# Graph attention, four layers: columns laid out by bits, marks of 0 and -1 as the penalty, and another order of the row tiles

## The reference

```
Wh = x @ W                                  # 4096 x 64
e = leaky(Wh @ a_src [:, None] + Wh @ a_dst [None, :])
scores = where(adj > 0, e, very negative)
out = softmax(scores, axis=1) @ Wh          # + bias in layer 1, elu in layers 0, 2, 3
x = layernorm(x + out)
```

## Time and profile before

| | |
|---|---|
| median of three runs | 632.23 us |
| the profiled execution | 631.51 us |
| its span, first to last instruction | 628.5 us |
| flag set, end of preparation | 216.00 us in the span |
| VectorE busy in the span | 426.0 us (68%) |
| GpSimd busy | 355.6 us (57%) |
| adjacency loads | 32 of 2048 KB |
| gathers | 340 |

### The profile page before, as it was taken

How to read it: one execution, slowest core, us unless ns; L and a number is a source line. 1 busy time by engine, 2 the same in 40 slices (tenths; PEclk the granted TensorE clock), 3 DMA queues, 4 the chain that set the end, 5 groups by cost and what they waited for, 6 DMA issues and landing times.

```text
span 628.5 us, 10864 instructions
## 1 busy us (share of the span) xinstructions
PE 358.2 (57%) x3424; PEld 318.5 (51%) x3424; DVE 426.0 (68%) x1856; ACT 364.8 (58%) x797; POOL 355.6 (57%) x354
## 2 busy tenths in 40 slices
PE   2363422313321279985189777527977762797773
PEld 1252311212221279884179776427867652786663
DVE  2898879899999845898135667713566761356686
ACT  3564865767664067985067657407766740675573
POOL 0200476266675740006777777767777777777770
PEclk9999999999999999998589879858997975998796
DMA  7996999999992110001122222212222221222220
GB/s 264 429 395 260 360 377 403 422 409 411 409 405 79 26 16 1 19 19 48 33 27 28 37 46 45 46 32 28 29 37 44 46 46 30 28 38 35 44 38 29
DMA packets 22083, 86.73 MB, mean 138 GB/s; under 512 B 6851, under 2 KB 12102, under 8 KB 17798
## 3 DMA queue, kind: packets, MB, share of 16 engines
q1 hardware_dynamic: 10102, 73.40, 29.0%
q0 software_dynamic: 10880, 11.51, 12.9%
q10 hardware_dynamic: 1040, 1.08, 0.5%
HBM read 80.59 MB, written 5.37 MB: 137 GB/s over the span
## 4 chain that ended last, share of the span: by engine, by line
POOL 32%; DVE 18%; issue 12%; PE 7%; ACT 4%; DMA 2%; POOLq 0%; DVEq 0%; ACTq 0%
POOL xg L404 32%; PE bank L601 2%; PE bank L575 2%; DVE key L1106 2%; DVE arena L1079 1%; DMA xg<-table,index 1%; DVE stats L1131 1%; ACT arena L716 1%; DVE nbr L879 1%; DMA table<-wh 1%; DVE mean_var L1134 1%; DVE key L1128 1%; DVE penalty L999 1%; ACT arena L734 1%; DVE key L1115 1%
## 5 line engine op out<-in xcount | busy, mean ns | idle before, releaser
L404 POOL DMA_INDIRECT xg<-table,index x340 | 333.9, 982 | 172.6 <-issue 100.7
L716 ACT ACTIVATE arena<-bank,sloped_own 128x256 f32<-128x256 f32 (+3 forms) x144 | 76.9, 537 | 150.1 <-PE bank L575 149.6
L1079 DVE CUSTOM_DVE_ANT_0 arena<-bank,arena 128x256 f32<-128x256 f32 (+3 forms) x144 | 71.5, 499 | 132.5 <-ACT arena L716 132.0
L690 ACT ACTIVATE arena<-arena,half 128x4096 bf16<-128x4096 int32 x32 | 118.4, 3707 | 46.9 <-DMA arena<-in_adj_t 46.3
L575 PE MATMUL bank<-packed,xg 128*128 128x128 f32 x744 | 120.0, 300 | 0.0
L575 PEld LDWEIGHTS bank<-packed,xg 128*128 128x128 f32 x744 | 113.2, 216 | 2.3
L601 PE MATMUL bank<-xg,arena 128*128 128x64 f32 x744 | 105.2, 280 | 11.6 <-ACT arena L734 11.0
L601 PEld LDWEIGHTS bank<-xg,arena 128*128 128x128 f32 x744 | 98.6, 202 | 17.2 <-ACT arena L734 16.5
L572 PE MATMUL bank<-penalty,ident_b 128*128 128x256 bf16 (+3 forms) x144 | 48.7, 338 | 75.6 <-DMA xg<-table,index 70.9
L725 ACT ACTIVATE arena<-arena,neg_max 128x256 f32<-128x256 f32 (+3 forms) x144 | 81.2, 564 | 0.3 <-DVE neg_max L1088 0.3
L588 PE MATMUL bank<-packed,arena 128*128 128x128 f32 x372 | 65.9, 284 | 10.2 <-ACT arena L734 9.1
(11 more groups left out here) (128 smaller groups left out, 522.4 us busy)
## 6 DMA issues: line engine op xcount, KB each, us to landing
arena<-in_adj_t SPq DMA_DIRECT2D x32, 2048.0 KB, 12.2
xg<-table,index POOLq DMA_INDIRECT x340, 2.8
table<-wh SPq DMA_DIRECT2D x24, 132.0 KB, 1.9
table<-wh ACTq DMA_DIRECT2D x1, 1056.0 KB, 4.7
x<-in_x SPq DMA_DIRECT2D x1, 1024.0 KB, 10.5
out_x<-x SPq DMA_DIRECT2D x8, 128.0 KB, 1.9
slot_row<-in_c_slot_row SPq DMA_DIRECT2D x1, 384.0 KB, 10.7
packed<-in_c_packed SPq DMA_DIRECT2D x1, 359.0 KB
```

What stands on the lines that cost most here:

```text
L404: pool.indirect_dma_start(out=xg[:, c, :], out_offset=None, in_=table[l][0:rows, :], in_offset=bass.IndirectOffsetOnAxis(ap=index[:, c:c + ...
L690: nc.scalar.activation(masks[:, t % 2, :], arena[:, t % 3, :], ACT.Sign, bias=half[:, :]).then_inc(mask_made, 1)
L716: nc.scalar.activation(score[:, n % RING, 0:m * P], score_ps[n % len(score_ps)][:, 0:m * P], ACT.Relu, bias=sloped_own[:, k:k + 1], scale= ...
L1079: nc.vector.tensor_tensor_reduce(out=y, in0=score_ps[n % len(score_ps)][:, 0:m * P], in1=y, scale=1.0, scalar=MASKED, op0=ALU.add, op1=ALU ...
```

## The change

- **The order of the batches.** Tiles 20-23 and 24-27 come first, then tile 0, then 1-3 and the rest as before. `GATHER_START` stays 2, which is now tile 0's batch.
- **The layout of columns.** The transposed adjacency is arranged on the host so that bit b of word w is column 256 b + w of the table's order. The count becomes three columns of each code group (low, high, all), so that a group is 11 wide in place of 9. For parted tiles VectorE sums two of the three over all 32 groups.
- **Candidates without column numbers.** The word gets a mark (bit 30) by one OR, and one AND with `bit_mask` puts mark, bit and word into a value whose order as a float is that of the columns. GpSimd's product (L398) and VectorE's L972 are gone. After the picking three small instructions turn the values into columns: `above`, `bit_col` and `col`.
- **Marks.** `slot_rows` makes `off_row` of 0 (the row's slot) and -1 (not): one comparison and one `scalar_tensor_tensor` a tile, one and three for parted tiles. It is kept for all batches and serves as the penalty itself: the matmul at the start of a segment takes `wall` (1e30 on the diagonal) and `off_row`. The penalty pass (L999) is gone. In `lists` each matmul becomes two, one with ones and one with `off_row`.

```diff
-BATCHES = [(0, 1), (20, 4), (24, 4), (1, 3), (4, 4), (8, 4), (12, 4), (16, 4), (28, 2), (30, 2)]
+BATCHES = [(20, 4), (24, 4), (0, 1), (1, 3), (4, 4), (8, 4), (12, 4), (16, 4), (28, 2), (30, 2)]
...
-                nc.gpsimd.tensor_tensor(colv[:, 0:places * BITS].rearrange("p (r b) -> p r b", b=BITS),
-                                        word_f[:, 0:places].unsqueeze(2).broadcast_to(wide),
-                                        bit_next[:, :].unsqueeze(1).broadcast_to(wide), ALU.add).then_inc(col_made, 1)
...
-                            t = nc.tensor.matmul(list_ps[q % 2][:, (c - c0) * w:(c - c0 + 1) * w],
-                                                 inrow[:, at:at + P],
-                                                 nbrh[:, b % 2, (k - k0) * w:(k - k0 + 1) * w],
-                                                 start=(k == tiles[0]), stop=(k == tiles[-1] and k0 >= PARTED))
+                            nc.tensor.matmul(dst, ones_b[:, :], rows, start=(k == tiles[0]), stop=False)
+                            t = nc.tensor.matmul(dst, off_row[:, at:at + P], rows, start=False,
+                                                 stop=(k == tiles[-1] and k0 >= PARTED))
...
-                    nc.tensor.matmul(bank[:, 0:m * P], ident_b[:, :], penalty[:, at:at + m * P],
+                    nc.tensor.matmul(bank[:, 0:m * P], wall[:, :], off_row[:, at:at + m * P],
...
-                    nc.vector.tensor_reduce(deg_part[:, 0, j:j + 1], both[:, 0:LOW, WORDS_C], AX, ALU.add)
-                    done(nc.vector.tensor_reduce(deg_part[:, 1, j:j + 1], both[:, LOW:TILES, WORDS_C], AX, ALU.add), j)
+                    nc.vector.tensor_reduce(deg_part[:, 0, j:j + 1], both[:, :, WORDS_C], AX, ALU.add)
+                    done(nc.vector.tensor_reduce(deg_part[:, 1, j:j + 1], both[:, :, WORDS_C + 1], AX, ALU.add), j)
...
-                        nc.vector.tensor_scalar(begun[:, at:at + w], slot_row[:, 0:w], first[:, j:j + 1], 0.0,
-                                                ALU.add, ALU.is_gt)
-                        t = nc.vector.tensor_scalar(ended[:, at:at + w], slot_row[:, 0:w], last[:, j:j + 1], 0.0,
-                                                    ALU.add, ALU.is_gt)
-                    link(t)
-                    return nc.vector.tensor_tensor(dst[:, 0:total], begun[:, 0:total], ended[:, 0:total], ALU.subtract)
+                        if rest is None:
+                            t = nc.vector.tensor_scalar(out, slot_row[:, 0:w], edges[:, j:j + 1], 1.0, ALU.is_lt, ALU.add)
+                        else:
+                            t = nc.vector.scalar_tensor_tensor(out=out, in0=slot_row[:, 0:w], scalar=edges[:, j:j + 1],
+                                                               in1=rest[:, at:at + w], op0=ALU.is_lt, op1=ALU.subtract)
+                    return t
...
+                if k0 < PARTED:
+                    link(mark(sooner, 0, low_start))
+                    link(mark(off_low, 0, low_end, sooner))
+                    link(mark(sooner, 0, start, off_low))
+                else:
+                    link(mark(sooner, 0, start))
+                mark(off_row, PLACE[k0] * P, end, sooner).then_inc(slots_made, 1)
...
-                nc.vector.tensor_scalar(lane_of[:, 0:places], topi[:, 0:places], GROUP - 1, None, ALU.bitwise_and)
-                done(nc.vector.tensor_scalar(word[:, 0:places], topi[:, 0:places], WORDS - GROUP, 4,
-                                             ALU.bitwise_and, ALU.logical_shift_left))
+                done(nc.vector.tensor_scalar(topi[:, 0:places], topi[:, 0:places], MARK, None, ALU.bitwise_or))
                 ready()
-                done(nc.vector.tensor_tensor(word_f[:, 0:places], word[:, 0:places], lane_of[:, 0:places],
-                                             ALU.add), None, word_made)
-                done(nc.vector.tensor_tensor(bitv[:, 0:places * BITS].rearrange("p (r b) -> p r b", b=BITS),
+                done(nc.vector.tensor_tensor(cand[:, 0, 0:places * BITS].bitcast(I32).rearrange("p (r b) -> p r b", b=BITS),
...
-                v.wait_ge(col_made, b + 1)
-                done(nc.vector.scalar_tensor_tensor(out=cand[:, 0, 0:places * BITS], in0=bitv[:, 0:places * BITS],
-                                                    scalar=0.0, in1=colv[:, 0:places * BITS], op0=ALU.is_gt,
-                                                    op1=ALU.mult), None, col_used)
...
+                done(nc.vector.tensor_scalar(above[:, 0:places], nbr[:, 0:places], -2.0, None, ALU.add))
+                ready()
+                done(nc.vector.tensor_scalar(bit_col[:, 0:places], above[:, 0:places].bitcast(I32), 15, 0xFF00,
+                                             ALU.logical_shift_right, ALU.bitwise_and))
+                ready()
+                done(nc.vector.scalar_tensor_tensor(out=col[:, 0:places], in0=nbr[:, 0:places].bitcast(I32),
+                                                    scalar=WORDS - 1, in1=bit_col[:, 0:places],
+                                                    op0=ALU.bitwise_and, op1=ALU.bitwise_or))
...
-                nc.vector.tensor_scalar(penalty[:, PLACE[k0] * P:PLACE[k0 + n] * P],
-                                        inrow[:, 0:(PLACE[k0 + n] - PLACE[k0]) * P], 1.0, -MASKED,
-                                        ALU.subtract, ALU.mult).then_inc(penalty_made, 1)
```

More of the change, by code:

```diff
@@ L191, in gat_kernel @@
         topi = sb("topi", [P, MAXB], I32)
[L192 to L196, removed]
+        above = sb("above", [P, MAXB], F32)
+        bit_col = sb("bit_col", [P, MAXB], I32)
+        col = sb("col", [P, MAXB], I32)
         cand = sb("cand", [P, 2, MAXB * BITS], F32)
@@ L207, in gat_kernel @@
         from_end = sb("from_end", [P, TILES], F32)
[L208 to L212, removed]
+        sooner = sb("sooner", [P, MAXBC * P], BF16)
+        off_low = sb("off_low", [P, MAXBC * P], BF16)
+        off_row = sb("off_row", [P, PLACE[TILES] * P], BF16)
+        wall = sb("wall", [P, P], BF16)
         rank = sb("rank", [P, 2, MAXBC], F32)
@@ L804, in _ @@
             v.wait_ge(loaded, 16 * NLOAD)
-            for dst, src in [(packer, packer_f), (fix, fix_f), (ones_b, ones), (before, before_f), (ident_b, ident)]:
-                t = nc.vector.tensor_copy(dst[:, :], src[:, :])
-            t.then_inc(cast_made, 1)
+            for dst, src in [(packer, packer_f), (fix, fix_f), (ones_b, ones), (before, before_f)]:
+                nc.vector.tensor_copy(dst[:, :], src[:, :])
+            nc.vector.tensor_scalar(wall[:, :], ident[:, :], -MASKED, None, ALU.mult).then_inc(cast_made, 1)
             for a in range(2):
@@ L894, in slot_rows, with mark @@
                     v.wait_ge(slots_loaded, 32)
[L895 removed]
+                def mark(dst, place, edges, rest=None):
                     for j in range(n):
[L898 to L911 removed]
+                        w = CHUNKS[k0 + j] * P
+                        at = (PLACE[k0 + j] - PLACE[k0]) * P
+                        out = dst[:, place + at:place + at + w]
+                        if rest is None:
[4 more added lines that the diff above has]
+                    return t
+                start, end = from_start[:, k0:k0 + n], from_end[:, k0:k0 + n]
+                if k0 < PARTED:
+                    link(mark(sooner, 0, low_start))
[4 more added lines that the diff above has]
+                mark(off_row, PLACE[k0] * P, end, sooner).then_inc(slots_made, 1)
             def list_neighbours(b):
@@ L982, in list_neighbours @@
                     ready()
-                    done(nc.vector.tensor_scalar(found[:, 0, 0:room], nbr[:, 0:room], 0.0, None, ALU.is_gt))
+                    done(nc.vector.tensor_scalar(found[:, 0, 0:room], nbr[:, 0:room], NO_BIT, None, ALU.is_gt))
                     ready()
@@ L990, in list_neighbours @@
                 ready()
-                done(nc.vector.tensor_scalar(lists_h[:, :, 0:room], nbr[:, 0:places].rearrange("p (t r) -> p t r", r=room),
-                                             float(-1 - CENTER), None, ALU.add), None, nbr_made)
+                done(nc.vector.tensor_scalar(above[:, 0:places], nbr[:, 0:places], -2.0, None, ALU.add))
[6 more added lines that the diff above has]
+                                                    op0=ALU.bitwise_and, op1=ALU.bitwise_or))
+                ready()
+                done(nc.vector.tensor_scalar(lists_h[:, :, 0:room], col[:, 0:places].rearrange("p (t r) -> p t r", r=room),
+                                             float(-FIRST_COL - CENTER), None, ALU.add), None, nbr_made)
             def pick_neighbours(b):
@@ L1258, in _constants @@
     packed = [np.eye(P), np.ones((P, P)), p[:, None] < p[None, :], packer, slot,
-              rows(np.arange(MAXR)), rows(GROUP * np.arange(BITS) + 1), rows([0.5 - o for o in OFFSET]),
-              rows(ROOM + [-(OFFSET[k] + UNITS[k] * UNIT) for k in range(TILES)] +
```

(6 more changed lines are left out.)

88 lines of the change are left out of this document (41 added, 47 removed).

## The result

The changed kernel takes 645.73 us, median of four runs (644.89 to 647.52), against 632.5 us for the kernel before (four runs, 631.78 to 633.42): a ratio of 1.0212, with an interval of 1.0186 to 1.0239. The forecast was 639.0 with a range of 629 to 643. The direction was right, the size was not: the loss is twice the one forecast, and the time lies outside the range.

A forecast was written before the change was run, and what follows sets the result against it. VectorE was taken to bound preparation, loads following closely: tile 0's start at 70.5 plus 152.3 us of work put the flag at 222.8, 6.8 us later; added to the median 632.23 that gave 639.0 us, range 629 to 643.

The forecast's parts named there:

- When VectorE can start tile 0 after the change: Preparation: after eight cheap turns and the batch of tiles 24-27, VectorE starts tile 0 at 70.5 us.
- What is left for VectorE from there, part by part: VectorE's work from tile 0's start to the flag: 165.5 us of old work becomes 152.3 us.
- The marks: VectorE's slot marks: scalar_tensor_tensor at 1.22 us per 1024 elements replaces comparison and subtraction; +0.5 us over the 8 batches.
- penalty pass: VectorE's pass making the penalty, 12.3 us in 8 instructions, goes; about 0.8 overlapped or lay in a wait: -11.5 us.
- `above`, `bit_col`, `col` and the lists' column: Three dependent small VectorE instructions a batch after the picking, about 0.22 us each in 8 batches: +5.3 us.
- picks of tile 0: VectorE's picking of tile 0, done before 84.36 us in the old kernel, now comes behind tile 0's list: +6.7 us.
- small instructions beside GpSimd: Small VectorE instructions slowed beside GpSimd's column product, counted outside the penalty passes, get faster as it goes: -3.5 us.
- Whether it waits: End of preparation: last mask can start at 205.3, its code comes 3 us before VectorE asks, so VectorE stays the bound.
- Layers unchanged: The four layers after the flag keep their time; a change of over 1 us would make the prediction wrong.
- The first: Marks run at two elements a cycle, the loads become the bound: 632.5 to 634 us, say 633; chance 0.18.
- The second rival: Marks at two elements a cycle and faster loads after the stall: 628 us, far form near 622; chance 0.14 together.
- third rival: Denser gathers slow the loads to 5.8 us each, last code at 215 or later: 641 to 643 us; chance 0.08.

The follow-up runs named there:

- the two experiments that gave it less and more to do: Changed kernel with marks as a comparison and one 16-bit subtraction per batch: 643.67 us; changed kernel with the penalty pass added back into scratch: 650.05 us.

## Why the prediction was wrong

The flag was forecast as 70.5 + 152.3 = 222.8. It is 71.2 + 159.0 = 230.2. The mechanism was as foreseen (tile 0 late, all work behind it late); what failed is the size of the work. Step by step, with the steps as the prediction names them:

- **"When VectorE can start tile 0 after the change": right.** 71.18 for 70.5, code 7 at 63.28 for 63.0.
- **"What is left for VectorE from there, part by part": this step failed**, by 6.7 us, and by its sizes, not by its mechanism. Most of it is one term, **"The marks", forecast +0.5, measured +4.15** (30.45 us before, 34.60 after, start to start). The rate taken from the 1024 form, 1.22 us, was right, and so was tile 0's part (1.82 us an instruction for 1.75). The sum over the 8 batches was not. At 1.04 ns an element, 1.22 and 1.75 us both leave some 0.15 us for the instruction itself. From tile 0 on the instruction stands 40 times, 12 of them only 256 wide: 20,400 elements x 1.04 ns + 40 x 0.15 us are 27.2 us, and 27.2 were measured. The forecast +0.5 leaves it 23.5 (30.45 + 0.5, less 7.45 for the comparisons), under 0.1 us for the instruction itself. So the prediction's own numbers for one instruction would have given about +4. Its working shows tile 0 alone, at 1536 elements, the width at which the fixed part shows least; in the sum over the batches that part is missing by half or more.
- The other terms of that step: penalty pass -11.7 (forecast -11.5), L972 -8.75 (-8.7), lane, word and their sum -1.8 (-2.0), `above`, `bit_col`, `col` and the lists' column +6.0 (+5.3), picks of tile 0 +6.6 (+6.7): right within 0.7 each. Of the 3.5 us for small instructions beside GpSimd, `low_end` gave 2.2, and no rows show the rest. The cast in front of the OR on `topi` (+0.4), the sums of degrees (+0.25) and more short waits for TensorE (+0.8), "under 1 us a batch, beside VectorE's work", were priced at nothing. These small ones are 3 us together, all on one side: what is added in small pieces costs its steps, and I rounded them down.
- **"Whether it waits": right in its answer, wrong in its numbers.** VectorE hardly waits: 0.29 and 0.19 us, at 198.65 and at the last code. But the last mask starts at 215.22, not 205.3. I followed the masks only through tile 0's hold and let the loads run freely after it. In fact a VectorE that is behind holds them again (138.07, 162.41), since a pack needs its codes read. The loads ran freely from 182 us on only, each mask then waiting for its load, and where that run began was VectorE's doing. The end was a near tie, 0.2 us, and the margin of 3 us on which I leaned was not there. That VectorE's side of it is the bound rests on the two experiments that gave it less and more to do.
- **Layers unchanged: right**, 412.8 for 412.5.
- **The rivals.** The first falls with 1.82 us for 1536 elements. The sentence of the Trainium skill in the Vector Engine (DVE) Microarchitecture Reference, section "Points that are easy to get wrong", must not be read the other way: with 16-bit sources this instruction is not faster, here at one element in 1.05 ns. The wide sources took 1.22 us for 1024, the same rate. The second rival needed the first. The third foresaw a longer stall, through the gathers; the stall was longer, through VectorE, and with a third fewer gathers the time did not move.
- **The range** ended at 643 by the third rival alone. An error of 4% in a sum of 165 us is 7 us; the upper end should have held that.

## What to carry to other kernels

Moving the dearest piece of the bounding engine's work behind cheap ones makes everything behind it late when that engine idles until it comes: with that order the start of the piece plus the work left was the end, in three kernels and with work taken off or added. Price a fused elementwise instruction by an element's part and an instruction's part, from rows of two widths where there are two, and count the second as often as it is issued. Producer transfers that are throttled by the consumer's buffers are not an independent second bound: follow them through every hold, not through the first.

## What the runs showed of the hardware

- scalar_tensor_tensor with 16-bit sources and result: 0.479 us for 256 elements, 1.82 for 1536, one element in 1.05 ns and 0.2 us besides; the comparison of 1536 took 0.62.
- The 16-bit pass over a batch's marks averages 0.47 us by itself and averaged 1.54 in the kernel with GpSimd's product; the five long ones there ended 0.3 to 0.5 us after the product did.
- Gathers beside loads at over 380 GB/s: with two a turn in place of three, the last seven masks came every 5.21 us in place of 5.55 in the new order, and the last one 1.4 us earlier; in the old order it came 0.5 us earlier.
- On two chips the four kernels run there took 646 to 675 us after the flag instead of 411 to 414, with an ordinary preparation, and the kernel before took 894 and 886 us in all; not explained.
